# Router and low-rank down product merged over alternating PSUM banks, up product one output tile later, four output banks

## The reference

```python
xc       = einsum('bsi,boi->bso', x, weight[ids])        # "cond"
logits   = xc @ W_router.T                               # 8 experts
probs    = softmax(logits); keep the two largest, renormalise -> combine
h        = einsum('nd,erd->ner', xc, A_stack) * combine  # 8 experts x rank 16 = 128 rows
lora_out = einsum('ner,eor->no', h, B_stack) * 2.0
out      = x + xc @ W_base.T + b_base + lora_out
```

## Time and profile before

| what | us |
|---|---|
| median of 3 runs | 437.0 |
| lowest and highest run | 435.49, 439.32 |
| span of the profiled execution | 435.4 |
| TensorE busy in it | 420.7 |

### The profile page before, as it was taken

One profiled execution on the slowest core, in us unless ns is written; L12 is line 12 of the kernel. 1 busy time (PEld: TensorE's weight loads), 2 busy tenths in 40 slices (PEclk: granted clock), 3 DMA queues, 4 the chain that ended last, 5 costly groups with the idle time before them and its releaser, 6 DMA issues.

```text
span 435.4 us, 5595 instructions
## 1 busy us (share of the span) xinstructions
PE 420.7 (97%) x2080; PEld 352.7 (81%) x2080; DVE 201.3 (46%) x328; ACT 142.6 (33%) x240; POOL 1.9 (0%) x7
## 2 busy tenths in 40 slices
PE   2999979999999999999999999999999999999996
PEld 2888858888888888888888888888888888888885
DVE  3687867233268785211137777411105874241102
ACT  4677743110057672000017665000004764110000
POOL 1000000000000000000000000000000000000000
PEclk9999999999999999999999999999999999999999
DMA  6786863244548575022225677202233760001222
GB/s 214 281 290 226 299 227 117 96 146 171 188 162 299 195 249 190 0 76 94 72 96 206 231 231 247 96 24 96 73 96 111 253 218 1 2 0 64 82 96 97
DMA packets 26982, 64.37 MB, mean 148 GB/s; under 512 B 2594, under 2 KB 10802, under 8 KB 26962
## 3 DMA queue, kind: packets, MB, share of 16 engines
q1 hardware_dynamic: 26848, 63.97, 43.4%
q0 software_dynamic: 112, 0.14, 0.1%
HBM read 55.71 MB, written 8.39 MB: 147 GB/s over the span
## 4 chain that ended last, share of the span: by engine, by line
PE 86%; DVE 5%; DMA 5%; SPq 2%; ACT 2%; issue 0%
PE ps_base L508 15%; PE ps_base L510 15%; PE ps_base L509 15%; PE ps_cond L543 10%; PE ps_cond L545 5%; PE ps_logit L543 5%; PE ps_h L543 5%; DVE wc_hl L385 3%; PE ps_logit L545 3%; PE ps_h L545 3%; DMA raw<-w_cond 2%; PE ps_h L508 2%; PE ps_logit L557 2%; PE ps_h L509 2%; PE ps_logit L558 2%; PE ps_h L510 2%
## 5 line engine op out<-in xcount | busy, mean ns | idle before, releaser
L508 PE MATMUL ps_base<-xc_hl,wb_hl 128*128 128x512 f32 x256 | 100.2, 391 | 0.0
L510 PE MATMUL ps_base<-xc_hl,wb_hl 128*128 128x512 f32 x256 | 99.7, 389 | 0.0
L509 PE MATMUL ps_base<-xc_hl,wb_hl 128*128 128x512 f32 x256 | 99.6, 389 | 0.0
L543 PE MATMUL ps_cond<-x_hl,wc_hl 128*128 128x512 f32 x256 | 91.0, 398 | 0.3 <-DVE wc_hl L385 0.3
L480 DVE SCALAR_TENSOR_TENSOR out_sb<-ps_base,bias_sb,out_sb 128x512 f32<-128x512 f32 x32 | 23.7, 750 | 140.2 <-PE ps_base L510 140.2
L385 DVE TENSOR_TENSOR wc_hl<-raw,wc_hl 128x1024 fp32r<-128x1024 f32 x62 | 75.7, 1222 | 23.1 <-ACT wc_hl L329 23.1
L545 PE MATMUL ps_cond<-x_hl,wc_hl 128*128 128x256 f32 x256 | 71.7, 280 | 0.0
L329 ACT CAST wc_hl<-raw 128x1024 fp32r<-128x1024 f32 x62 | 65.2, 1051 | 8.2 <-DMA raw<-w_cond 8.2
L543 PEld LDWEIGHTS ps_cond<-x_hl,wc_hl 128*128 128x128 f32 x256 | 48.1, 188 | 12.4 <-DVE wc_hl L385 0.6
L510 PEld LDWEIGHTS ps_base<-xc_hl,wb_hl 128*128 128x128 f32 x256 | 48.0, 188 | 10.2
L509 PEld LDWEIGHTS ps_base<-xc_hl,wb_hl 128*128 128x128 f32 x256 | 48.1, 188 | 10.0
(11 more groups left out here) (72 smaller groups left out, 350.9 us busy)
## 6 DMA issues: line engine op xcount, KB each, us to landing
raw<-w_cond SPq DMA_DIRECT2D x62, 512.0 KB, 4.4
out_sb<-x SPq DMA_DIRECT2D x32, 256.0 KB, 3.0
out<-out_sb SPq DMA_DIRECT2D x32, 256.0 KB, 2.0
raw<-x SPq DMA_DIRECT2D x14, 512.0 KB, 3.6
raw<-w_base SPq DMA_DIRECT2D x8, 512.0 KB, 4.0
raw<-x SPq DMA_DIRECT2D x4, 256.0 KB, 3.3
raw<-w_cond SPq DMA_DIRECT2D x4, 256.0 KB, 4.4
raw<-lora_a SPq DMA_DIRECT2D x1, 512.0 KB, 5.8
```

Source lines behind the costliest of these rows:

```text
L508: nc.tensor.matmul(ps, w_hi, v_hi, start=start, stop=False)
L509: nc.tensor.matmul(ps, w_hi, v_lo, start=False, stop=False)
L510: return nc.tensor.matmul(ps, w_lo, v_hi, start=False, stop=stop)
L543: nc.tensor.matmul(ps[:], wc_hl[:, w, HI, k], x_hl[:, s, k].rearrange("p h n -> p (h n)"), start=(k == 0), stop=False)
```

## The change

The router and the down product become one loop over k, in which the matmuls go alternately to ps_logit and ps_h. The logits' transposes move from the middle of the down product to k = 3 of `base(0)`. The gate's transposes move from behind `base(0)` to behind `base(1)`. `lora_up(o)` follows `base(o + 2)` instead of `base(o + 1)`. The output tiles rotate over four banks; the fourth is ps_cond2, so that `cond` waits for all outputs of the pair before at its tile t = 2. The programs of ACT, SP and GpSimd and the order of DVE's program are unchanged.

```diff
+BASES = 4
-        ps_base = [psum(f"ps_base{i}") for i in range(3)]
+        ps_base = [psum(f"ps_base{i}") for i in range(BASES - 1)]
         ps_cond = [ps_logit, ps_h, psum("ps_cond2"), psum("ps_cond3")]
+        ps_base.append(ps_cond[2])
@@ DVE
-                        ... ps_base[o % 3][:] ...
+                        ... ps_base[o % BASES][:] ...
@@ cond
+                    if not first and s == 0 and t == 2:
+                        pe.wait_ge(out_done, p * KT)
@@
-            def router(p, first):
-            def lora_down(p, first):
+            def router_and_down(p, first):
                 if first:
                     pe.wait_ge(wr_split, 1)
+                    pe.wait_ge(lo_done, split_at[("a", 0, 0)] + 1)
                 for k in range(KT):
                     if k == 0 or k == KT - 1:
                         pe.wait_ge(xc_lo, p * (2 * KT) + KT + (KT - 1 if k == 0 else KT))
                     w = wr_hl[:, k * NR:k * NR + P]
+                    start, stop = k == 0, k == KT - 1
+                    nc.tensor.matmul(ps_logit[:], w, xc_hl[:, k, HI], start=start, stop=False)
+                    nc.tensor.matmul(ps_h[:], a_hl[:, HI, k], xc_hl[:, k, HI], start=start, stop=False)
+                    logits = nc.tensor.matmul(ps_logit[:], w, xc_hl[:, k, LO], start=False, stop=stop)
+                    if stop:
+                        logits.then_inc(router_done, 1)
+                    nc.tensor.matmul(ps_h[:], a_hl[:, HI, k], xc_hl[:, k, LO], start=False, stop=False)
+                    down = nc.tensor.matmul(ps_h[:], a_hl[:, LO, k], xc_hl[:, k, HI], start=False, stop=stop)
+                down.then_inc(h_done, 1)
+            def logits_to_tokens():
+                for q in range(NQ):
+                    tok = nc.tensor.transpose(tok_parts[:, q], logit_t[:, q * P:(q + 1) * P], ident[0:NR, 0:NR])
+                tok.then_inc(tok_done, 1)
@@ base
-                if o >= 3:
-                    pe.wait_ge(out_done, p * KT + o - 2)
+                if o >= BASES:
+                    pe.wait_ge(out_done, p * KT + o - BASES + 1)
                 for k in range(KT):
+                    if o == 0 and k == 2:
+                        pe.wait_ge(logit_copied, p + 1)
+                        if first:
+                            pe.wait_ge(consts_in, 16)
+                    if o == 0 and k == 3:
+                        logits_to_tokens()
-                    product(ps_base[o % 3][:], ...
+                    product(ps_base[o % BASES][:], ...
@@ body
-                router(p, first)
-                lora_down(p, first)
+                router_and_down(p, first)
                 base(p, first, 0)
+                base(p, first, 1)
                 pe.wait_ge(gate_ready, p + 1)
                 ...
-                for o in range(1, KT):
+                for o in range(2, KT):
                     base(p, first, o)
-                    if o == 1:
+                    if o == 2:
                         if first:
                             pe.wait_ge(lo_done, split_at[("b", 0, 0)] + 1)
                         pe.wait_ge(h_split, p + 1)
-                    lora_up(o - 1)
+                    lora_up(o - 2)
+                lora_up(KT - 2)
                 lora_up(KT - 1)
```

More of the change, by code:

```diff
@@ L479, in body @@
                         dve.wait_ge(res_in[o % OUTS], p * (16 * (KT // OUTS)) + 16 * (o // OUTS + 1))
-                        nc.vector.scalar_tensor_tensor(out_sb[:, o % OUTS], ps_base[o % 3][:], bias_sb[:, o:o + 1],
+                        nc.vector.scalar_tensor_tensor(out_sb[:, o % OUTS], ps_base[o % BASES][:], bias_sb[:, o:o + 1],
                                                        out_sb[:, o % OUTS], ALU.add, ALU.add).then_inc(out_done, 1)
@@ L556, in router @@
                     w = wr_hl[:, k * NR:k * NR + P]
-                    nc.tensor.matmul(ps_logit[:], w, xc_hl[:, k, HI], start=(k == 0), stop=False)
-                    mm = nc.tensor.matmul(ps_logit[:], w, xc_hl[:, k, LO], start=False, stop=(k == KT - 1))
-                mm.then_inc(router_done, 1)
-            def lora_down(p, first):
[L562 to L577, removed]
+                    start, stop = k == 0, k == KT - 1
[11 more added lines that the diff above has]
+                tok.then_inc(tok_done, 1)
             def base(p, first, o):
@@ L583, in base @@
                     pe.wait_ge(out_done, p * KT)
-                if o >= 3:
-                    pe.wait_ge(out_done, p * KT + o - 2)
+                if o >= BASES:
+                    pe.wait_ge(out_done, p * KT + o - BASES + 1)
                 for k in range(KT):
-                    product(ps_base[o % 3][:], wb_hl[:, o, HI, k], wb_hl[:, o, LO, k],
+                    if o == 0 and k == 2:
[4 more added lines that the diff above has]
+                        logits_to_tokens()
+                    product(ps_base[o % BASES][:], wb_hl[:, o, HI, k], wb_hl[:, o, LO, k],
                             xc_hl[:, k, HI], xc_hl[:, k, LO], k == 0, False)
             def lora_up(o):
-                product(ps_base[o % 3][:], b_hl[:, HI, o], b_hl[:, LO, o], h_hl[:, HI], h_hl[:, LO],
+                product(ps_base[o % BASES][:], b_hl[:, HI, o], b_hl[:, LO, o], h_hl[:, HI], h_hl[:, LO],
                         False, True).then_inc(base_done, 1)
```

## The result

The changed kernel takes 468.84 us (median of 4 runs, 467.9 to 469.51) against 438.16 us for the kernel before, measured beside it. The ratio is 1.070, 95% interval 1.066 to 1.075: **7% slower**. The forecast was 456.5 us with a range to 461.5; the direction was right, the size was not. The profiled execution has a span of 467.3 us, 31.9 more than before. In what follows a run over 1.5% above the fastest of its kernel is left out of the medians.

A forecast was written before the change was run, and what follows sets the result against it. TensorE, busy 97% at full clock, was taken to bound the kernel, so only pace or idle stretches count. Waits of 3.0 + 11.2 + 4.4 + 0.9 + 0 (pace) = 19.5 us on 437.0 gave 456.5 us, range 453.0 to 461.5.

The forecast's parts named there:

- Part 2: Moved transposes: in pair 0 base(1) waits once for its LO split behind the gate on DVE, 3.0 us.
- Part 3: Up product one tile later: base(3) to base(7) of pair 0 wait 2.23 us each for splits, 11.2 us.
- Part 4: End of a pair: residual of tile 7 comes late, 4.4 us at kernel end, nearly hidden between pairs.
- Part 1: Router and down product in one loop: changing banks costs and saves nothing, 0 us, bounds 2.2 us either way.
- rival A: TensorE's new waits bring its clock down, about 2 us per drop: 458.5 for one, 468.5 for six; chance 8%.
- the start of a pair: Next pair's cond waits on the previous pair's late tile 7: 0.3 us for each of three, 0.9 us.
- The wait at t = 2: In cond, for the previous pair's output tile 7: about 0.1 us, taken as 0.3, bounds 0 and 1.5 each.
- rival B: Pair starts: new weight loads come late, TensorE waits about 1.5 us in each of three pairs, 461; chance 12%.
- the prediction's own signs of being wrong: Pair 0 waits absent or under 1 us, matmuls after them at 0.64 us pace, pairs 1 to 3 changing over 1 us each.
- full in all 40 slices: Whole kernel before: the prediction's reading that TensorE's granted clock is full throughout the profiled span.

The follow-up runs named there:

- experiment 2: Changed kernel, but in pair 0 the two splits of W_base's tile 1 stand ahead of the gate on ACT and DVE: 464.3 us.
- the last two experiments: experiment 9, and the kernel of experiment 8 run again on the same chip: 437.3 us and 434.6 us.
- experiment 9: Kernel before, its two loops kept, but waiting for xc's late tiles at the k that reads them: 437.3 us, ratio 0.997.
- experiment 6: Changed kernel, but in pair 0 base(3) to base(7) start with four matmuls needing only the HI part, then wait for LO: 457.9 us.
- Experiment 3: Changed kernel, but output tile 7 has its own buffer (h_sb's memory), its residual loaded at output tile 0: 461.0 us.
- experiment 4: Changed kernel with the edits of experiment 1, experiment 2 and Experiment 3 together: 439.17 us, ratio 1.0024 to the kernel before.
- experiment 1: Changed kernel, but in pair 0 the split of W_base's tile o + 3 (not o + 2) stands at step o: 451.5 us, ratio 1.031.
- experiment 8: Kernel of experiment 4, but the merged loop waits for xc's late tiles only at the k that reads them: 435.5 us, ratio 0.994.

## Why the prediction was wrong

**Right: which waits come, where and how long.** Part 2 (wait ahead of base(1)) was 3.0 us and measured 2.93. Part 3 (five waits on VectorE's queue) was 11.2 and measured 10.65. Part 4 at the end of the kernel was 4.4 and measured 5.1; the residual took 3.65 us from issue to use, not 3.0. Part 1 was 0; alternation, restarts and the rest of pairs 1 to 3 made 0.5. Experiments 1 to 4 show these causes by taking each away: their times are met within 0.9 us, by a theory that takes the terms from the profile after (experiment 2 in part by chance, as said there).

**Wrong: rival A, given 8%, happened.** The step that failed is the sentence "after the 3.21 us wait in pair 0 the matmuls run at their full pace ..., and the new waits are shorter". It took one row for a rule, and so the slow matmuls behind the waits stood in the sum at nothing; they measured 9.6 us. The runs show that a wait of that length may or may not bring TensorE to 1.2 GHz. This seems to hold in the kernel before too: its mean granted clock is 0.996 in 26 of the 54 runs beside the experiments and 0.999 or 1.000 in the others. Beside the last two experiments the 12 runs at 0.996 lie at 438.2 to 439.9 us, the five at 1.000 at 436.6 to 438.2. A stretch at half pace that loses 1.6 us in 437 is just that 0.004. No profile of such a run of the kernel before was kept; that of experiment 9, also at 0.996, has one slow stretch behind its wait at the router's last step. The profile of before is one at 1.000.

In the twelve profiles of this case, a wait of 1.78 to 3.25 us in pair 0 was followed by the slow pace 26 times of 31: behind the router's wait 6 of 8, behind the 2.8 us wait ahead of base(1) 5 of 5, behind the 1.98 us waits 15 of 18. Waits of up to 1.25 us were never followed by it once TensorE had come to its full pace (five in experiment 6, and those at the router and in cond). Between 1.25 and 1.78 us there is no such case, and what decides after a wait of 1.98 us is not shown: in the changed kernel base(3) passed, in experiment 2 none did. The changed kernel has six slow stretches. The price in rival A, about 2 us each, was somewhat high against 1.6. That its sum of 468.5 for six drops is the measured time to 0.3 us is luck: one of the six new waits was followed by none, the sixth stretch stands behind the old wait at the router, and what the price has too much the other terms had too little. What was wrong was its chance.

**A smaller miss: the start of a pair.** 0.9 us was forecast for three pairs and 2.75 measured. The wait at t = 2 was mis-sized, since the residual took longer, and the restart was left out. The rest is near to rival B, though not by its way: TensorE never waited for a weight in pairs 1 to 3, but it waited at the router for VectorE's split of xc, 0.41 us in pair 2; that VectorE was still behind from the start of the pair is the likely reason, not one shown by itself. Pairs 1 and 2 became 1.4 and 1.5 us longer, which was one of the prediction's own signs of being wrong; matmuls at the slow pace behind the waits were another. Experiment 3 shows that all 2.75 us hang on the residual of tile 7.

By the spans: 454.9 forecast, and 10.4 (clock, with five restarts) + 1.85 (starts of pairs) + 0.7 (end) + 0.5 (pace) - 0.6 (waits) - 0.6 (start of the kernel) + 0.15 (restart of base(3)) is the 12.4 us to 467.3.

The Trainium skill (TensorE: Matmul & The Clock Gate, section HAM oscillation — how this bites in real kernels) tells of a kernel whose waits between bursts of matmuls throttle TensorE again and again, and whose work behind each wait then runs cold. The waits told of there are for transfers and of some 3 to 5 us. The trace agrees in kind, and with shorter waits: four of the five base tiles behind a wait of 1.98 us run at a granted clock of 0.76.

## What to carry to other kernels

When work on the bound engine is moved later, look at what stands *behind its consumer* in the other engines' queues: here every split of the next weights stood behind the output of an earlier tile, so that a shift by one tile put it on the path five times. Price a new idle stretch on TensorE at its length and at the slow matmuls behind it, and do not take one good row as proof that there will be none; look at the spread of the runs and their mean clock beside the one profile. Two loops that are merged help where the inputs of their last steps come late, if the waits are put at the step that needs them (here 0.6% to 0.9%).

## What the runs showed of the hardware that was not expected

- Idle stretches of 1.8 us can be enough to bring TensorE to its lower level for some time: in experiment 4 a wait of 1.80 us cost 1.6 us more in the matmuls behind it. The same wait can go unpunished: 1.78 us in experiment 1, 3.21 us in the earlier trace rows.
- The drop need not start with the first matmul after the wait. After 102.24 the first two steps take 0.34 and 0.26 us, and the next ones 0.43 each. In experiment 2 the slow pace is there from the first on (89.23 to 89.67).
- At the start of a kernel the granted clock of the windows can't be relied on: in experiment 8 the 17 matmuls from 11.92 to 17.02 us run at 0.64 us for a pair of 512 and 256 columns, the slow pace as in the earlier trace rows, and the window shows 1.00. So "full in all 40 slices", as the prediction read the earlier trace rows, does not hold for the first two (in the kernel before the slow pace lasts from 8.3 to 12.2 us); the distance between starts tells it.
- Changing the PSUM bank from matmul to matmul cost about 2 ns each here (9.24 against 9.16 us for 40) and gave nothing; the same 40 matmuls also stand in another order, and the two are not told apart.
